# Slot one-hots by four comparisons, and the first dense block of each later pass with its early tiles first

## The reference

```python
def _segment_sum(src, seg, n):
    return jax.ops.segment_sum(src, seg, n)
...
h = jnp.maximum(_layernorm(x, axis=-1), 0.0)
x = x + _L0_gnn_ref(h, ...)   # two layers, each: agg = segment_sum((h @ W0 + b0)[src], dst); concat with h @ W1 + b1; @ W2; / std
x = x + _L1_gnn_ref(...)      # segment_sum(x[src] @ W + b) / degree
x = x + _L2_gnn_ref(...)      # three layers, each: segment_sum((h @ W)[src] * dinv[src] * dinv[dst])
x = x + _L3_gnn_ref(...)      # messages relu(e @ Wm1) @ Wm2 of e = [h[src], h[dst]], times edge_attr_96, segment_sum, node network
```

## Time and profile before

| | |
|---|---|
| runs (3) | 7778.75, 7788.18, 7788.41 us |
| median | 7788.18 us |
| profiled execution | 7780.93 us |
| its span, first to last instruction | 7779.1 us |
| TensorE busy in it | 6960.1 us (89%) |
| POOL busy | 5398.6 us (69%) |
| VectorE busy | 3609.6 us (46%) |
| ScalarE busy | 1612.6 us (21%) |

### The profile page before, as it was taken

One profiled execution on the slowest core, in us unless ns is written; L12 is line 12 of the kernel. 1 busy time (PEld: TensorE's weight loads), 2 busy tenths in 40 slices (PEclk: granted clock), 3 DMA queues, 4 the chain that ended last, 5 costly groups with the idle time before them and its releaser, 6 DMA issues.

```text
span 7779.1 us, 139548 instructions
## 1 busy us (share of the span) xinstructions
PE 6960.1 (89%) x53778; PEld 5623.6 (72%) x53778; DVE 3609.6 (46%) x7497; ACT 1612.6 (21%) x3217; POOL 5398.6 (69%) x5559
## 2 busy tenths in 40 slices
PE   2999999899989999999999999999987777777787
PEld 1677777787777777777877777777766666666676
DVE  7888988334442333333322333333344444444444
ACT  4777777111110000000000000010111111111111
POOL 0466666677657777677767777677747777777776
PEclk9999999999999999999999999999988999899898
DMA  7334333666565666655665556666545555555554
GB/s 152 116 129 133 132 123 132 187 191 188 182 200 185 198 196 192 206 183 181 191 207 179 185 186 188 205 193 187 185 154 148 146 146 148 143 151 145 149 144 131
DMA packets 568381, 1306.54 MB, mean 168 GB/s; under 512 B 223636, under 2 KB 326359, under 8 KB 560471
## 3 DMA queue, kind: packets, MB, share of 16 engines
q1 hardware_dynamic: 295076, 810.67, 31.5%
q0 software_dynamic: 177744, 371.65, 18.5%
q10 hardware_dynamic: 94948, 115.60, 4.3%
HBM read 1097.44 MB, written 207.42 MB: 168 GB/s over the span
## 4 chain that ended last, share of the span: by engine, by line
PE 53%; POOL 19%; issue 8%; DMA 3%; DVE 3%; ACT 0%; ACTq 0%; SPq 0%; DVEq 0%; POOLq 0%
PE PS L2451 41%; POOL GF L826 19%; PE PS L2431 5%; DMA work<-amat 2%; PE PS L2598 1%; PE PS L2297 1%; PE PS L2306 1%; PE PS L2516 1%; PE PS L2438 1%; PE PS L2316 0%; PE PS L2293 0%; PE PS L2457 0%; PE PS L2292 0%; DVE work L1839 0%; PE PS L2295 0%
## 5 line engine op out<-in xcount | busy, mean ns | idle before, releaser
L2451 PE MATMUL PS<-PARTS,work 128*128 128x288 bf16 x27930 | 3617.2, 288 | 66.9 <-issue 44.9
L2451 PEld LDWEIGHTS PS<-PARTS,work 128*128 128x128 fp8e4 x27930 | 2747.0, 99 | 760.2 <-issue 83.0
L837 POOL DMA_INDIRECT GF<-newparts,SRC x1640 | 1563.5, 953 | 687.9 <-issue 493.9
L837 POOL DMA_INDIRECT work<-newparts,SRC x1655 | 1576.7, 953 | 540.6 <-issue 498.3
L826 POOL DMA_INDIRECT GF<-table,SRC x1563 | 1475.0, 944 | 532.5 <-issue 475.7
L821 POOL DMA_INDIRECT GF<-newparts,SRC x659 | 749.9, 1138 | 505.0 <-PE PS L2538 202.1
L2598 PE MATMUL PS<-PARTS,work 128*128 128x289 bf16 x5586 | 999.0, 289 | 0.0
L1190 ACT ACTIVATE work<-PS 128x396 fp8e4<-128x396 f32 x1824 | 865.5, 500 | 290.3 <-PE PS L2516 246.2
L1913 DVE TENSOR_REDUCE FREE<-PS 128x96 f32<-128x288 f32 x415 | 189.7, 457 | 1431.1 <-PE PS L2431 1419.1
L2378 PE MATMUL PS<-work,QW 128*96 128x512 bf16 x1173 | 395.9, 455 | 427.8 <-DMA GF<-table,SRC 388.6
L1839 DVE TENSOR_TENSOR work<-PS,REL 128x1024 bf16<-128x1024 f32 (+1 forms) x611 | 741.3, 1214 | 0.3 <-issue 0.3
(11 more groups left out here) (293 smaller groups left out, 5892.0 us busy)
## 6 DMA issues: line engine op xcount, KB each, us to landing
work<-amat SPq DMA_DIRECT2D x285, 896.0 KB
work<-amat SPq DMA_DIRECT2D x285, 672.0 KB
work<-in_dst_dram SPq DMA_DIRECT2D x195, 512.0 KB
amat<-work SPq DMA_DIRECT2D x57, 1568.0 KB, 5.8
work<-in_edge_attr_dram SPq DMA_DIRECT2D x195, 384.0 KB
GF<-newparts,SRC POOLq DMA_INDIRECT x2299
PARTS<-newparts SPq DMA_DIRECT2D x35, 1008.0 KB, 10.0
work<-newparts,SRC POOLq DMA_INDIRECT x1655
```

The costliest lines, as they stand in the source:

```text
L837: pool.indirect_dma_start(GP[place_of(g)][:, i, :], None, part_rows[a % 2], bass.IndirectOffsetOnAxis(ap=SRC[:, tile:tile + 1], axis=0)).t ...
L2451: last = pe.matmul(PS[:, dense_bank(d), 0:PQ], AB[m][:, jj * WIN:(jj + 1) * WIN].bitcast(FP8), PARTS[:, j * PQ:j * PQ + PQ], start=(j == 0 ...
```

## The change

Two things. In the first pass, the slot one-hots are made by four comparisons of 128 float16 columns with a float32 column each, in place of one comparison of 512 with a broadcast float16 row; the slot numbers stay float32. In the dense passes, block 0 is taken in two goes: first its 85 early tiles (all but 50 to 55 and 91 to 97), in dense passes 3 to 5 already between the last units' products and transposes, then pieces 0 to 2 of block 1, then the 13 late tiles. The loads are split to suit: the early tiles of pieces 3 and 6 come with the other parts, the late ones when all is stored; block 1 comes as pieces 0 to 2, piece 3, and pieces 4 to 6, all ahead of the degrees.

```diff
+EARLY = {3: (42, 50, 56), 6: (84, 91, 98)}
-        SLOT16 = [BT[:, c, 0:P // 2].bitcast(F16) for c in range(2)]
...
+            def load_part_tiles(a, t0, t1, landed):
+                sp.dma_start(PARTS[:, t0 * PQ:t1 * PQ], newparts[a % 2][:, t0 * PQ:t1 * PQ]).then_inc(landed, 16)
...
                     for m in range(AC):
                         sp.wait_ge(d_mm, a * DB * AC + m + 1)
-                        if m not in (3, 6):
+                        if m in EARLY:
+                            load_part_tiles(a, EARLY[m][0], EARLY[m][1], p_ld[m])
+                        else:
                             load_parts(a, (m,))
                         for first, n in LOADS:
                             if m == first + n - 1:
                                 load_pieces(0, a * DB, first, n)
+                    load_pieces(1, a * DB, 0, 3)
                     if a < 3:
                         sp.wait_ge(S["uns"], done(S, "uns", a))
                     sp.wait_ge(S["par"], 16 * done(S, "par", a))
-                    load_parts(a, (3, 6))
+                    for m in EARLY:
+                        sp.wait_ge(p_ld[m], 32 * a - 16)
+                        load_part_tiles(a, EARLY[m][1], EARLY[m][2], p_ld[m])
+                    load_pieces(1, a * DB, 3, 1, d_ld[0])
+                    load_pieces(1, a * DB, 4, 3)
...
-                    with sp.Fori(1, DB) as d:
+                    with sp.Fori(2, DB) as d:
                         load_block(d, a * DB)
...
-                to = BT[:, c % 2, P:2 * P] if n else SLOT16[c % 2]
+                to = BT[:, c % 2, n * P:(n + 1) * P]
...
-                slots = SLOT16[c % 2][:, 4 * q % P:4 * q % P + 4]
-                last = dve.tensor_tensor(PRING[:, 4 * q % RING:4 * q % RING + 4, :],
-                                         IO16[:, 0:P].unsqueeze(1).to_broadcast([P, 4, P]),
-                                         slots.unsqueeze(2).to_broadcast([P, 4, P]), ALU.is_equal)
+                for w in range(4 * q, 4 * q + 4):
+                    last = dve.tensor_scalar(PRING[:, w % RING, :], IO16[:, 0:P], BT[:, c % 2, w % P:w % P + 1], None,
+                                             ALU.is_equal)
...
                 for half in range(HALVES):
                     product(s, phase, half, u, own=not begun)
+                if begun is not None and name in ("l1", "l2a", "l2b"):
+                    early_tiles(phase)
...
+            def early_tiles(a):
+
+                b0 = a * DB
+                pe.wait_ge(d_add, b0 + 1)
+                for m in range(AC):
+                    if m == 0:
+                        pe.wait_ge(d_ld[0], 16 * ((a - 1) * (DB + 1) + 1))
+                    if m == 4:
+                        pe.wait_ge(d_ld[4], 16 * ((a - 1) * DB + 1))
+                    pe.wait_ge(p_ld[m], 32 * a - 16 if m in EARLY else 16 * a)
+                    pe.nop(nofuse=True)
+                    last = tile_sums(0, m * piece_tiles, EARLY[m][1] if m in EARLY else (m + 1) * piece_tiles)
+                    if m < 3:
+                        last.then_inc(d_mm, 1)
...
+                def first_blocks():
+
+                    pe.wait_ge(p_ld[3], 32 * a)
+                    tile_sums(0, EARLY[3][1], EARLY[3][2]).then_inc(d_mm, 1)
+                    pe.wait_ge(p_ld[6], 32 * a)
+                    tile_sums(0, EARLY[6][1], EARLY[6][2]).then_inc(d_mm, 3 + PIECES_FIRST - AC)
...
+                        if p == 0 and a < 3:
+                            early_tiles(a)
+                        if d == 0:
+                            continue
...
-                        piece(d, m)
+                        last = piece(d, m)
+                        if p >= PIECES_FIRST:
+                            last.then_inc(d_mm, 1)
+                        elif p == PIECES_FIRST - 1:
+                            first_blocks()
```

More of the change, by code:

```diff
@@ L584, in _, with load_pieces @@
                              t[name][0:P * (TPG - TAIL_TILES)].rearrange("(p i) -> p i", p=P)).then_inc(s_edges, 16)
-            def load_pieces(d, b0, m, n):
+            def load_pieces(d, b0, m, n, landed=None):
                 sp.wait_ge(d_mm, d * AC + (b0 * AC + m + n))
@@ L589, in load_pieces @@
                 sp.dma_start(AB_BYTES[:, m * ACW:(m + n) * ACW], amat_rows[bass.ds(d * P, P), m * ACW:(m + n) * ACW]
-                             ).then_inc(d_ld[m], 16)
+                             ).then_inc(d_ld[m] if landed is None else landed, 16)
             def load_block(d, b0):
@@ L2318, in halves, with last_units @@
                 last.then_inc(S["pq"], 1)
-            def last_units(s, phase, begun=False):
+            def last_units(s, phase, begun=None):
                 name, u = PHASES[phase], TURNS - 1
@@ L2417, in all_groups, with tile_sums @@
                         window_sums(0, rows, x_sum)
+            piece_tiles = NT // AC
+            def tile_sums(d, first, end):
+                for j in range(first, end):
+                    m, jj = divmod(j, piece_tiles)
+                    last = pe.matmul(PS[:, dense_bank(d), 0:PQ], AB[m][:, jj * WIN:(jj + 1) * WIN].bitcast(FP8),
+                                     PARTS[:, j * PQ:j * PQ + PQ], start=(j == 0), stop=(j == NT - 1))
+                return last
+            def early_tiles(a):
[11 more added lines that the diff above has]
+                        last.then_inc(d_mm, 1)
             def with_dense(a):
                 g0, b0 = a * GG, a * DB
-                piece_tiles = NT // AC
                 def gathered(t):
@@ L2440, in piece @@
                 def piece(d, m):
-                    if m in LOADED:
-                        pe.wait_ge(d_ld[m], d * 16 + (b0 - DB + 1) * 16)
                     if m == 0:
+                        pe.wait_ge(d_ld[0], 16 * ((a - 1) * (DB + 1) + d + 1 + (d > 1)))
                         pe.wait_ge(d_add, d + b0)
-                    if d == 0:
-                        pe.wait_ge(d_add, b0 + 1)
-                        pe.wait_ge(p_ld[m], 16 * a)
+                    if d == 1 and m == 3:
+                        pe.wait_ge(d_ld[0], 16 * ((a - 1) * (DB + 1) + 3))
+                    if m == 4:
+                        pe.wait_ge(d_ld[4], 16 * ((a - 1) * DB + d + 1))
                     pe.nop(nofuse=True)
[L2449 to L2453, removed]
+                    return tile_sums(d, m * piece_tiles, (m + 1) * piece_tiles)
+                def first_blocks():
[3 more added lines that the diff above has]
+                    tile_sums(0, EARLY[6][1], EARLY[6][2]).then_inc(d_mm, 3 + PIECES_FIRST - AC)
                 def turn_sums(d):
```

## The result

The kernel before took 7782.07 us (median of 15 runs, 7772.24 to 7788.41), the changed one 7796.11 us (median of 15, 7791.81 to 7813.4): a ratio of 1.0021, interval 1.0014 to 1.0027, some 14 us slower. The time lies in the range that was forecast; the forecast of no measurable change does not hold. The profiled execution took 7794.64 us with a span of 7792.8, against 7780.93 and 7779.1.

What follows compares the result with a forecast made beforehand. The prediction took TensorE as bound in the first pass and dense pass 1, GpSimd's gathers in passes 2 to 4 and until late in 5. Terms +4 - 7 + 4 - 1 = 0 gave 7788 us, range 7772 to 7812.

Steps and rivals of the forecast that it cites:

- a stall of TensorE before block 2: Dense pass 1: a TensorE wait of about 9 us before block 2, in place of the one before block 1.
- The pauses: GpSimd between dense passes: its idle time before each next pass's gathers grows by about a microsecond.
- Part 1: First pass, new one-hot comparisons: +0.10 us a quad on VectorE, of which +4 us reaches TensorE; bounds -13 and +48.
- its own rule: First pass: each of TensorE's 20 waits for one-hots grows by two quads' addition, 20 x 2 x 0.10 = +4 us.
- an addition below that is mostly taken by idle time: First pass: VectorE's 0.22 us a quad of idle time for ring slots mostly absorbs any smaller addition.
- VectorE becomes the bound: First pass, slower rival: additions beyond 0.22 us a quad cost 438 quads each; up to +48 us, about 7835; chance 0.13.
- Part 2: Head of dense pass 1: early tiles first, stall moved by one block, block 2 at 1448.6 against 1455.85: -7 us.
- a second limit: Dense pass 1, group 16: the gathers allow no more than 15.3 us less the landing, about 12, of gain.
- The reading of the old stall: Dense pass 1 before the change: TensorE's 9.86 us stand, block 1 being loaded behind the round trip of the degrees.
- Part 3: Heads of passes 2 to 5: early loads delay the last units' transfers, 3 x 1.3 = +4 us (0 to +8).
- the piece that it left to a rival: Three pass transitions: block 1's load delays stores, 1.6 us each, with early loads +13 for +4, about 7798; chance 0.05.
- Pass 5: Dense pass 5: the 0.96 us wait at 5071.53 only grows; some spread of the landings may give -1 us.

## Why the forecast failed, by its own steps

Nearly all that was to show the forecast right did show: unbroken gathers in passes 2 to 4, a stall of TensorE before block 2 (5.92 us, and 3.04 for the group ahead of it, 9 in all as forecast), a step of 0.16 us, 36.7 us of waits for one-hots. Each of these is a sign of the mechanism; none of them carries the sizes. The pauses did not: they were to grow by about a microsecond each and grew by 0.9, 5.3 and 2.0.

**Part 1, forecast +4, measured +10.6.** The six kernels with the old one-hots ended the first pass at 1375.0 to 1380.8 us (mean 1378.6), the three with the new ones at 1388.1, 1390.8 and 1388.9 (mean 1389.3). The price of an instruction was right (0.65 us built from rows, 0.65 measured; with the surcharge for running gathers the forecast took +0.10 a quad, where the rows show 0.05 to 0.06, by which its own rule gives +2). What failed is the step "an addition below that is mostly taken by idle time": the 0.22 us of idle time a quad are not a reserve. VectorE may begin a quad only when the quad two before it is built whole, so that idle time which falls early cannot be saved up for a burst of node work later, and TensorE's waits grow in number (24 to 43) more than in length. The rows for this were at hand and read on the wrong line: the matmul's idle time (33.3 us) in place of the weight load's (40.6 us), whose growth followed the pass in every variant (+10.4, +38.2, +93.2 and -18.6 us for +7, +38, +103 and -26). The rival "VectorE becomes the bound" had the place right and the point from which it decides wrong: at 0.21 us a quad, still below that point, four tenths of the addition came through. The formula in the errata section of the page "VectorE: DVE Perf Modes" in the Trainium skill, by which four comparisons would take an estimated 0.38 us, does not fit: 0.65 was measured; the section itself says that the formula is too low for a single operation.

**Part 2, forecast -7, measured about -3.** From last gather to last gather, pass 1 took 886.9 to 891.1 us in five kernels with the old head (mean 888.6) and 883.8 to 887.4 in five with the new (mean 885.8). The moved stall is there, and block 2 came 4.4 us earlier against the end of the first pass, not 7. What the step left out: the early part loads also hold up the stores of the last parts, so that GpSimd starts 3.3 us later (pause 39.4 in place of 36.1 in the mean of eight and six kernels), and TensorE waits 5.1 us ahead of the first two groups. That the gathers set a second limit was right, and they set it nearer. The reading of the old stall was wrong too: of its 9.86 us the degrees' round trip was the smaller part, and the rest stayed when the round trip was out of the way.

**Part 3, forecast +4, measured +9.** GpSimd's pauses from pass 2 to 5 are 69.3 to 75.1 us in nine kernels that load as before (mean 73.3) and 79.5 to 85.1 in four with the head (mean 82.4). The mechanism was the forecast's, transfers in the way of the last parts; the term +4 was mis-sized by half, and what came was its upper bound. One reason is the piece that it left to a rival: block 1's load in front of the stores. With that load behind the late parts the pauses are 77.8 in the one execution there is, so it may account for about half. The waits between store and load at the ends of passes 3 and 4 are 6.9 us together in the kernel before (6.3 to 8.5 in the nine) and 12.4 to 13.2 in the four with the head, some 5.5 us of the 9. The rest is that the stores themselves go out later after the last gather, by some 3.5 us in the mean over the three pauses. Part of this is TensorE at half clock between the last gather and the store: 2.42 us for ten products, 1.33 before, at the end of pass 4 in the second execution of the changed kernel. But the head in pass 1 alone shows the same at the end of pass 3, so that the head's share in it is not shown. The waits between store and load, 3.4 and 3.6 us before and 4.5 to 7.9 with the head, agree with a rule of the Trainium skill, page "DMA: Bandwidth & Descriptors", section "Queues, rings and completion order": the count that tells of a transfer lands only behind all earlier writes of the same DMA engine, across its queues.

**Pass 5, forecast -1.** Pass 5 took 861.6 us in place of 862.9; other kernels without the head had 859.7 to 868.9, so it can't be told.

The sum of the means is +10.6 - 2.8 + 9.0 = +17, the two measurements of the changed kernel gave +14 both times. The one-hots and the head, each alone, gave +6.3 and +0.8 by their medians; both intervals reach some 7 us to either side, so that the gap between these times and the rows is not settled.

## What to carry to other kernels

Do not count a producer's idle time behind a ring as a reserve: of additions of 0.05 and 0.21 us a quad, beside 0.22 of idle time, 0.3 to 0.4 came through here. Look at the grain in which slots are given back and handed over: one by one in place of four by four was worth some 30 us (6.3 us above and 23.4 below their own runs of before), twice what the whole change cost. Read a stall at the weight load, not at the matmul, when the late operand is the weights. Before moving loads ahead, look at which small store goes out behind them and who waits for it.

## What the hardware showed beside this

The gathers of the first pass got shorter with the new comparisons, from 1138 to 1071 ns in the mean of 659, 44 us in all, and nothing came of it, since GpSimd waits for TensorE there. The same happened in the one-hots alone (1074). With the old comparison back and the head kept, the mean was 1146, so it goes with the comparison. The Trainium skill, page "SBUF — State Buffer", section "SBUF: two separate sides", says that a VectorE operation in a two-port mode, or with two inputs in SBUF beside a GpSimd operation that reads SBUF, and the GpSimd operation exclude each other from a shared port. The times agree with it for the old comparison with its two tensor operands; they do not show the lock.

The same wait of TensorE can cost its clock or not. In pass 1 a wait for a ScalarE eviction was followed by the full 2.4 GHz in the changed kernel (after 2.40 us) and for the most part by 1.2 GHz with the head alone (after 2.39 us) (each row is a stretch of 8 us behind the wait, with busy time and count of each engine, granted clock, DMA share and GB/s):

```profile
1774.00:1782.00 8.00, 8.00 (x69) 6.76 (x69) 0.46 (x1) 0.21 (x1) 5.90 (x7) 1.00 0.56 168
```

```profile
1762.00:1770.00 8.00, 7.88 (x39) 6.80 (x40) 0.39 (x1) 0.74 (x1) 6.17 (x7) 0.57 0.37 97
```

The third number from the right is the clock, 1.00 and 0.57: 69 matmuls in the one stretch, 39 in the other. There are six such waits in pass 1. Over the five kernels that treat pass 1 alike it took 886.9 to 891.1 us; that the clock makes this scatter is likely but not shown.
